# Another order of the four instruction queues in the first part of a two-block graph network kernel

## The reference

```
h = max(layernorm(x), 0)
xp = h @ W_proj;  xh = xp split into 8 heads of 32
a_src, a_dst = xh . W_att[:, :32], xh . W_att[:, 32:]
scores = leaky_relu(a_src[i] + a_dst[j] + b_att, 0.2), -1e30 where adj == 0
x = x + relu(softmax(scores) @ xh)
h = max(layernorm(x), 0)          # what the second block starts from
x = x + three_layer_gnn(h, adj)   # the second part, not touched
```

## Time and profile before

| what | value |
|---|---|
| time, median of 3 runs | 1663.23 us (1660.30 to 1664.78) |
| the profiled execution's own time | 1663.78 us |
| its span, first to last instruction | 1662.0 us |
| granted TensorE clock, mean | 0.972 of 2.4 GHz |
| busy shares | TensorE 92%, VectorE 83%, ScalarE 65%, GpSimd 54% |
| end of the first part's last step | 347 us |

### The profile page before, as it was taken

One profiled execution on the slowest core, in us unless ns is written; L12 is line 12 of the kernel. 1 busy time (PEld: TensorE's weight loads), 2 busy tenths in 40 slices (PEclk: granted clock), 3 DMA queues, 4 the chain that ended last, 5 costly groups with the idle time before them and its releaser, 6 DMA issues. The chain is left out here.

```text
span 1662.0 us, 37278 instructions
## 1 busy us (share of the span) xinstructions
PE 1524.7 (92%) x11360; PEld 1282.6 (77%) x11360; DVE 1378.4 (83%) x4302; ACT 1087.1 (65%) x1946; POOL 891.4 (54%) x1008
## 2 busy tenths in 40 slices
PE   6888888827999999998999999899999999999995
PEld 6566666616888888887888888788888888888885
DVE  2889999967988989887888988888898888988852
ACT  1667777714677677665767666576777766677663
POOL 1667777723455355563545456444545656355464
PEclk9999999957999999999999999999999999999998
DMA  6233333250000011110001111100011211000001
GB/s 183 81 122 120 100 113 113 77 186 18 7 14 14 13 39 47 57 62 11 7 14 29 45 49 64 34 8 14 14 39 29 80 33 39 7 14 7 14 26 51
DMA packets 70894, 83.00 MB, mean 50 GB/s; under 512 B 29264, under 2 KB 54096, under 8 KB 70736
## 3 DMA queue, kind: packets, MB, share of 16 engines
q1 hardware_dynamic: 69104, 74.76, 15.2%
q0 software_dynamic: 816, 3.15, 0.6%
q10 hardware_dynamic: 816, 3.15, 0.5%
HBM read 38.95 MB, written 25.17 MB: 39 GB/s over the span
## 5 line engine op out<-in xcount | busy, mean ns | idle before, releaser
L805 ACT ACTIVATE bank<-bank,b_col 128x512 f32<-128x512 f32 x384 | 253.0, 659 | 365.2 <-PE bank L753 364.9
L765 PE MATMUL bank<-w_hi,hid_hi 128*128 128x256 f32 x1536 | 443.3, 289 | 17.8 <-DVE hid_lo L965 13.0
L765 PE MATMUL bank<-w_hi,hid_lo 128*128 128x256 f32 x1536 | 433.2, 282 | 0.0
L765 PE MATMUL bank<-w_lo,hid_hi 128*128 128x256 f32 x1536 | 432.8, 282 | 0.0
L965 DVE TENSOR_TENSOR hid_lo<-bank,hid_hi 128x512 fp32r<-128x512 f32 x384 | 259.1, 685 | 146.5 <-ACT hid_hi L810 143.0
L765 PEld LDWEIGHTS bank<-w_hi,hid_hi 128*128 128x128 f32 x1536 | 289.3, 188 | 53.8 <-DVE hid_lo L965 41.5
L753 PE MATMUL bank<-nT_hi,w_hi 128*128 128x512 f32 x768 | 318.2, 414 | 6.2 <-issue 4.8
L753 PE MATMUL bank<-nT_hi,w_lo 128*128 128x512 f32 x768 | 305.0, 397 | 4.8 <-issue 4.8
L753 PE MATMUL bank<-nT_lo,w_hi 128*128 128x512 f32 x768 | 304.0, 396 | 0.0
L765 PEld LDWEIGHTS bank<-w_lo,hid_hi 128*128 128x128 f32 x1536 | 289.6, 189 | 10.3
L765 PEld LDWEIGHTS bank<-w_hi,hid_lo 128*128 128x128 f32 x1536 | 289.4, 188 | 0.0
(11 more groups left out here) (122 smaller groups left out, 3076.9 us busy)
## 6 DMA issues: line engine op xcount, KB each, us to landing
x_other<-x_cur SPq DMA_DIRECT2D x96, 128.0 KB, 2.4
xin<-in_x_dram SPq DMA_DIRECT2D x16, 512.0 KB
first_block_out<-x_res SPq DMA_DIRECT2D x16, 512.0 KB
second_block_in<-x_act SPq DMA_DIRECT2D x16, 512.0 KB
x_cur<-second_block_in SPq DMA_DIRECT2D x16, 512.0 KB, 3.7
x_fin<-first_block_out SPq DMA_DIRECT2D x16, 512.0 KB, 3.6
out_dram<-x_fin SPq DMA_DIRECT2D x16, 512.0 KB, 2.9
xh_other<-xh SPq DMA_DIRECT2D x128, 33.0 KB, 1.9
```

Source lines behind the costliest of these rows:

```text
L765: mm = pe.matmul(FF[t // 2][:, (t % 2) * D:(t % 2 + 1) * D], a[:, r, t * P:(t + 1) * P], w[:, l, c, :], start=(c == 0 and t % 2 == 0 and p ...
L805: act.activation(h[:], h[:], ACT.Gelu, bias=b1_col[:, l, c:c + 1]).then_inc(s_gelu, 1)
```

## The change

In the first part's `step` of four queues the order of the operations is another one. Nothing is computed in another way, no buffer and no transfer is changed, and SyncE's queue is as before.

- TensorE: head products (L300), turning of `hrelu`, turning of `weights`, scores, projection. Before: `hrelu`, head products, `weights`, projection, scores.
- ScalarE: w1's high half, `xh`, w2's high half, `hT`, `weights_T`, `hrelu`, `scored`, exp, `x_act`.
- VectorE: `no_edge`, `stats` of xin, `leaky`, `stats` of x_res, `top`, the two `mv`, `src_hi`, `inv`, `neg`, `vare`, `shifted`, `headout`, `a_dst`, `src_lo`, w1's low half.
- GpSimd: w2's low half, `rstd` of this step's statistics (before: of the step before), w2's transfer, `x_res`, `dst_diag`, `nmr` of this step's statistics at the end.
- `leaky` has one more wait (`q_d`), `dst_diag` waits for the second of the three source and destination steps (before: the first), and `src_lo` for the first (before: the second), since `src_hi` now comes ahead of `a_dst`.

The core of the diff, for the two queues whose operations are split up most (the lines of TensorE and ScalarE are moved whole):

```diff
@@ GpSimd, step
-                    S, r = tau - 1, (t - 1)
+                    if splits_w2(tau):
+                        pool.wait_ge(s_whi, 4 * L + 1 + (tau - HEAD))
+                        pool.tensor_tensor(w2_part(w2_lo, tau), raw_part(tau),
+                                           w2_part(w2_hi, tau).bitcast(F32), ALU.subtract).then_inc(s_w2lo, 1)
+                    S, r = tau, t
                     if counted(S):
                         pool.wait_ge(q_mv, S + 1)
                         at_least(pool, q_act, S - 12)
                         pool.tensor_tensor(rstd[:, r % 4, :], vare[:, r % 4, :], minus_half[:, 0:2], ALU.pow).then_inc(q_rs, 1)
-                        pool.wait_ge(q_rs, S + 1)
-                        pool.tensor_tensor(nmr[:, r % 4, :], neg[:, r % 4, :], rstd[:, r % 4, :], ALU.mult).then_inc(q_nmr, 1)
...
-                        pool.wait_ge(q_asd, 3 * T + 1)
+                        pool.wait_ge(q_asd, 3 * T + 2)
...
+                    if counted(tau):
+                        pool.wait_ge(q_rs, tau + 1)
+                        pool.tensor_tensor(nmr[:, t % 4, :], neg[:, t % 4, :], rstd[:, t % 4, :], ALU.mult).then_inc(q_nmr, 1)
@@ VectorE, step
+                    T, r = tau - 4, (t - 4)
+                    if has(T):
+                        at_least(dve, q_bc, T - 1)
+                        dve.tensor_scalar(no_edge[:, r % 2], adjin[:, T % XR, :], 0.0, NEG, ALU.is_le, ALU.mult).then_inc(q_ne, 1)
...
+                        at_least(dve, q_d, scores)
...
+                    T, r = tau - 4, (t - 4)
+                    if has(T):
+                        dve.wait_ge(q_xh, T + 1)
+                        at_least(dve, q_bc, T - 3)
+                        dve.tensor_copy(src_hi[:, r % 4, :], bank[2 + r % 2][:, D:D + H]).then_inc(q_asd, 1)
+                    T = tau - 8
+                    if has(T):
+                        heads.unit(T)
+                        dve.wait_ge(q_ag, T + 1)
+                        G = heads2[:].rearrange("p e (h k) -> p (e h) k", k=P)
+                        heads.done(dve.reciprocal(inv[:].unsqueeze(2), G[:, :, HK:HC]))
+                    if counted(tau):
                         dve.wait_ge(q_mean, tau + 1)
                         dve.tensor_scalar(neg[:, t % 4].unsqueeze(2), mv[:, t % 4, :, 0:1], -1.0, None, ALU.mult)
                         dve.tensor_scalar(vare[:, t % 4].unsqueeze(2), mv[:, t % 4, :, 1:2], EPS, None, ALU.add).then_inc(q_mv, 1)
...
-                        dve.wait_ge(q_xh, T + 1)
                         at_least(dve, q_diag, 2 * (T - 3))
...
                         dve.tensor_tensor(a_dst[:, r % 4, :], X[:, D + H:D + 2 * H], batt_row[:], ALU.add).then_inc(q_asd, 1)
-                        at_least(dve, q_bc, T - 3)
-                        dve.tensor_copy(src_hi[:, r % 4, :], X[:, D:D + H]).then_inc(q_asd, 1)
-                        dve.wait_ge(q_asd, 3 * T + 2)
+                        dve.wait_ge(q_asd, 3 * T + 1)
                         dve.tensor_tensor(src_lo[:, r % 4, :], X[:, D:D + H], src_hi[:, r % 4, :].bitcast(F32),
                                           ALU.subtract).then_inc(q_asd, 1)
```

More of the change, by code:

```diff
@@ L278, in step @@
                         mm.then_inc(s_bias, 1)
[L279 to L287, removed]
                     T, r = tau - 8, (t - 8)
@@ L302, in step @@
                         mm.then_inc(q_ag, 1)
+                    T, r = tau - 2, (t - 2)
+                    if has(T):
+                        if isinstance(T, int) and T == 0:
+                            pe.wait_ge(s_const, 2)
+                        pe.wait_ge(q_h, T + 1)
+                        at_least(pe, q_hT, T - 1)
+                        for k in range(KD):
+                            mm = pe.transpose(bank[r % 2][:, k * P:(k + 1) * P], hrelu[:, r % 2, k * P:(k + 1) * P], ident[:])
+                        mm.then_inc(q_tr, 1)
                     T, r = tau - 7, (t - 7)
@@ L309, in step @@
                         mm.then_inc(q_wt, 1)
[L310 to L320, removed]
                     T, r = tau - 5, (t - 5)
@@ L335, in step @@
                                   start=False, stop=True).then_inc(q_bc, 1)
+                    T, r = tau - 3, (t - 3)
+                    if has(T):
+                        if isinstance(T, int) and T == 0:
+                            pe.wait_ge(s_su, 2 * KD * 2)
+                        pe.wait_ge(q_hT, T + 1)
+                        at_least(pe, q_xh, T - 1)
+                        at_least(pe, q_asd, 3 * (T - 1))
+                        for k in range(KD):
+                            mm = pe.matmul(bank[2 + r % 2][:, 0:WC], hT[:, r % 2, k * P:(k + 1) * P], wcat[:, k, :],
+                                           start=(k == 0), stop=(k == KD - 1))
+                        mm.then_inc(q_xp, 1)
                 steps(pe, step)
@@ L401, in step @@
                                        shifted[:].rearrange("p (e h) j -> p e h j", e=2), ACT.Exp).then_inc(q_e, 1)
+                    T, r = tau - 10, (t - 10)
+                    if has(T):
+                        act.wait_ge(q_nmr, T + 10)
+                        if r % 4 == 0:
+                            at_least(act, q_st, 8 * (T - 4))
+                        act.activation(x_act[:, T % 8, :],
+                                       x_res[:, T % 8, :], ACT.Relu,
+                                       bias=nmr[:, (r + 1) % 4, 1:2], scale=rstd[:, (r + 1) % 4, 1:2]).then_inc(q_act, 1)
                     if isinstance(tau, int) and tau == HEAD - 1:
@@ L500, in step @@
                                           b1_raw[:].rearrange("p l c -> p (l c)"), ALU.add).then_inc(s_b1, 1)
+                    scores = tau - 6
+                    if has(scores):
+                        score.unit(scores)
+                        dve.wait_ge(q_cp, scores + 1)
+                        at_least(dve, q_d, scores)
+                        score.done(dve.scalar_tensor_tensor(leaky[:], bank[4][:].rearrange("p (h j) -> p h j", h=H), SLOPE,
+                                                            scored[:], ALU.mult, ALU.max))
+                    if has(tau - 9):
+                        pause(dve, q_res, tau - 8, q_own)
+                        dve.bn_stats(stats[:, 1, :], x_res[:, (tau - 9) % 8, :]).then_inc(q_s1, 1)
                     if has(scores):
```

72 lines of the change are left out of this document (24 added, 48 removed).

## The result

The changed kernel takes 1619.9 us (median of four, 1618.86 to 1620.38), the kernel before beside it 1663.3. The ratio is 0.974, 95% interval 0.9724 to 0.9757: 43.4 us less. The prediction was 1648.4, with 1635 to 1666 as its range. The sign was right, the size was a third of the true one.

What follows compares the result with a forecast made beforehand. It took VectorE's queue, with `vare` held under `x_res`, to bound the loop. Steps of (3 x 4.08 + 4.62) / 4 = 4.21 against 4.51 save 14.4 us, the tail 1: 1663.8 - 14.4 - 1 = 1648.4 us, range 1635 to 1666.

Steps and rivals of the forecast that it cites:

- VectorE's string with the held `vare`: Loop, VectorE: 4.28 us a step, with `vare` held under `x_res` some 0.56 us in most steps; 3.63 after the change.
- The ring of VectorE and GpSimd: Loop: GpSimd's row after `headout`, 2.91 us, then `neg` to `headout`, 1.17; together 4.08 us, the ordinary step.
- The fourth step: Every fourth loop step: the branch delays `no_edge` until `x_res` holds it, 0.99 us more, a step of 4.62.
- TensorE's floor: Loop, TensorE: its own work sums to 3.96 us a step, and no order of it goes below that.
- The first rival: Loop: TensorE's floor is reached, with no ring of VectorE and GpSimd; 1636 us, chance 0.12.
- The head: First part ahead of the loop: GpSimd's wait to send for w2 is untouched; no gain, bounds 3 less and 6 more.
- `vare` at 0.16: Sign, VectorE's loop step: `vare` takes 0.16 us in every step, otherwise the main step is wrong.
- `neg` longer than when it is free: Sign, VectorE's loop step: `neg` takes longer than 0.17 us and ends with GpSimd's `w_lo`.
- the weights' wait gone: Sign, TensorE's loop step: the wait of 0.42 us for `weights` goes.
- The tail: End of the first part, 33.8 us: four of ten steps are full ones, 1 us less (0 to 2).
- The third rival: Loop: by the whole-instruction rule `rstd` holds `no_edge` 0.28 us; steps of about 4.4, 1658 us, chance 0.15.
- The second rival: Loop and head: `no_edge` is held in `vare`'s place in every step; 4.62 us a step, 1673 us, chance 0.15.

Runs made afterwards that it cites:

- e1: Kernel before with the two `mv`, `neg` and `vare` moved ahead of `shifted` in VectorE's queue, nothing else: 1668.66 us, ratio 1.0032.
- e11: Kernel before with only TensorE's and ScalarE's new orders, VectorE and GpSimd as before: 1644.68 us, ratio 0.9886.
- e15: Kernel before with only VectorE's and GpSimd's new orders, TensorE and ScalarE as before: 1673.17 us, ratio 1.0051.
- e3: Changed kernel with TensorE's queue put back in its old order: 1647.10 us, ratio 0.9908.
- e2: Kernel before with VectorE's whole new order, the other three queues old: 1717.24 us, ratio 1.0323.
- e14: Changed kernel with VectorE's queue put back in its old order: 1641.44 us, ratio 0.9870.
- e8: Changed kernel with one of the four score products of a step issued twice on TensorE: 1625.29 us, ratio 0.9768.

## Why the prediction was wrong

**What bounds the kernel before: the first step that failed.** The prediction took VectorE's string with the held `vare` as the loop's bound, because it was the one visible loss on a nearly full engine. e1 takes the hold away and is 5 us slower. Two rings lie close to that string, and what opens them are ScalarE's and TensorE's moves (e11), which the prediction put at nothing but a wait: the two-step ring through VectorE, GpSimd and ScalarE, 9.03 us for two steps, and the ring of scores, exp and weights through TensorE and ScalarE, 4.38. VectorE's own string, 4.28 to 4.53, is tied with the first. This error doesn't enter the sum, which starts from the measured 4.51, but it is why the forecast gave TensorE's and ScalarE's new orders no worth. e15, the part of the change that it was about, is no faster than the kernel before. The earlier trace rows had named the first one: a wait of over 1 us for `nmr` in nearly every step was read as idle time that hides, and it was a link of the ring.'s wait of 0.42 named the second.

**The ring of VectorE and GpSimd: mis-sized.** 4.08 was foretold, it is 3.80. The ring is the one that was foretold: `neg` does wait for the end of GpSimd's `w_lo`, and ends 0.03 us behind it (206.73 and 206.70). Two groups of its terms were too long. GpSimd's row was added up from durations, 0.73 + 1.18 + 0.20, where the starts lie 0.69, 1.14 and 0.15 us apart: 0.13. And from the end of `w_lo` to `shifted` 0.16 us were reckoned for `neg` and `vare`; `shifted` starts 0.01 behind it (206.71), since `vare` passes right behind the held `neg`: 0.15. Together 0.28 a step, or some 10 us over the three quarters of the loop's steps for which it was foretold. A second path was overlooked. It goes over `x_res` into `stats` of x_res, which now waits for it: from `headout` (203.51) to `x_res` 0.75, to `stats` 1.03 (at 205.29), to `headout` again 2.02 (207.31), 3.80 with the hold of `neg` in it and so nearly as long.

**The fourth step: mis-sized, from a row read wrongly.** 4.62 was foretold for it, 3.97 measured (the others 3.80 to 3.82). `no_edge` is 0.18 to 0.20 us there too; an idle time of 0.27 us falls behind it, ahead of `stats` of xin (212.09). The 0.53 us from `src_lo` to `leaky` in the earlier trace rows, taken for the loop's branch, is for the most part the wait for `scored` which the row itself names: at 211.91, with no end of the loop's body near, it is 0.50. (The body's end adds some 0.20: `leaky` starts 0.23 behind the end of `scored` at 225.67 and 0.03 behind it at 211.91.) The term is some 8 us of the loop's error.

**TensorE's floor: near, and the bound in the end.** 3.96 foretold, 3.85 measured. It was called a floor that "no order of this work goes below"; it was summed from the starts of the old order (in e3, which has that order, they come to 4.38 - 0.47 = 3.91). With the ring at 3.80 instead of 4.08, this string is the longer of the two and sets the mean step. The first rival (floor reached, 1636, chance 0.12) is right about the step, but not about the reason: the ring was not missing, and `neg` did not get in between two GpSimd instructions. The ring is only shorter than the floor. Its number came nearest because it was the lowest of all; for the head it had nothing either.

**The head: failed.** Nothing was foretold, with 3 less as the bound; it gave 9.9. The clock of 0.83 was seen and its cause named, but called untouched. The wait for `w_lo` in GpSimd's queue shrinks from 3.28 to 0.89 us, with this step's `rstd` now ahead of it and not behind, and TensorE's idle time from 2.00 to 1.14. Of the 9.9 us some 3.6 are this, 3.1 the new orders in the same stretch, and the rest lies around it.

**Right.** `vare` at 0.16; `neg` longer than when it is free, ending with `w_lo`; the weights' wait gone; `rstd` stretched to 1.05 by `shifted`. The tail was right in sign (1 foretold, at most 2, and 2.4 measured). The third rival, that `rstd` would shut VectorE out for a whole instruction, fell: `no_edge` (203.99, 0.18 us) runs at its usual length while `rstd` runs from 203.15 to 204.20. (`a_dst` and `src_lo` do so too, but they read one of their two tensors from PSUM, so they are no test of that rule.) The section "Who interferes with whom" of the Trainium skill's page "SBUF — State Buffer" holds here for `x_res` and `w_lo` as the holders, and not for this `rstd`. The second rival fell in the loop; in e3, with the scores late, `no_edge` was held as it says.

**The sum.** With the measured terms: loop 212.04 - 180.84 = 31.2, head 9.9, tail 2.4, second part 0.8, together the 44.3 that the span lost. The forecast had 14.4, 0, 1 and 0: the loop is short by 16.8, the head by 9.9.

## What to carry to other kernels

Take an idle time that recurs in every step for a link of a ring until it is shown to be slack: follow it around, through every queue and over as many steps as the trip takes, and divide. The loop's step is the longest of these quotients and of the engines' own strings; where several lie within a few per cent, as here 4.28, 4.38 and 4.51, an edit that shortens one of them can lose: both edits of VectorE's queue alone did (e1, e2), while e11, which opens the two rings and leaves the hold, gained 20 us. Add such a ring up from start to start, not from durations: the difference was 0.28 of 4.08 us here. A long instruction on a busy engine is a loss only if the ring goes over it: take it away first, as nearly alone as the order allows, and look.

## What was not expected of the hardware

A short stall can cost more than itself, and whether it does can't be told from its length in these runs. Behind TensorE's 2.00 us of idle time at 64.75 us the granted clock was 0.80 for five microseconds and 0.52 for the next five, the lower of its two levels (1.2 GHz) for nearly all of these, while the changed kernel's 1.14 us at the same place left it at 1.00. But e11 has a stall of 2.07 us in the same place (below), and its clock stays at 1.00 as well. In e14 the clock is 0.66 from 65 to 70 us, behind a stall of 2.07 us that ends at 64.89, and 1.00 behind one of 2.05 that ends at 84.59.

```profile
67.48 1.12 PE L323 MATMUL bank<-dst_diag,same_graph 128*128 128x512 f32 x2 [2.07 <-POOL dst_diag L452]
```

And a small instruction of VectorE is held for what is left of the GpSimd instruction that runs: `vare` for the whole 0.73 us of `x_res`, `neg` for the last 0.07 us of `w_lo` in the changed kernel and for 0.28 in e8. Beside `rstd`, a power of 128x2 numbers on GpSimd, `no_edge` and `vare` pass at their usual 0.18 and 0.16 us.
